# Moving the expert products of tile 0 into the last attention batch of a fused attention, product-key and two-gate expert kernel

## What is computed

```python
x = x + peer(attention(x, cond))          # layer 0
x = x + ffn(moe(x, cond))                 # layer 1
# peer: product keys
q   = batchnorm(a @ w_q)                  # statistics over all 2048 tokens
sim = q . keys                            # 2 x 8 heads x 32 keys for each token
# of the 32 x 32 sums of key scores of a head the best 8 are kept, softmax over them
h   = softmax(scores) * gelu(a @ down_embed[indices].T)
out = h @ up_embed[indices]
# moe: 8 experts, 3 layers, relu, top 2 of a softmax gate;  ffn: 8 experts, 2 layers, gelu, top 2 of a sigmoid gate
```

## Time and profile before

| | |
|---|---|
| median of 3 executions | 784.82 us |
| lowest, highest | 784.77, 787.23 us |
| profiled execution | 787.02 us |
| its span (first to last instruction) | 785.2 us, so 1.8 us lie around it |
| busy share of the span | PE 94%, PEld 83%, ACT 73%, DVE 71%, POOL 40% |
| stages in the span | attention to about 146 us; statistics and folded keys to 162; tiles 0 and 1 by products to 213; first turn to 265; turns in which PE never stops to 785 |

### The profile page before, as it was taken

How to read it: one execution, slowest core, us unless ns; L and a number is a source line. 1 busy time by engine, 2 the same in 40 slices (tenths; PEclk the granted TensorE clock), 3 DMA queues, 4 the chain that set the end, 5 groups by cost and what they waited for, 6 DMA issues and landing times.

```text
span 785.2 us, 14852 instructions
## 1 busy us (share of the span) xinstructions
PE 741.9 (94%) x5314; PEld 654.1 (83%) x5314; DVE 557.1 (71%) x1495; ACT 575.6 (73%) x1001; POOL 312.2 (40%) x214
## 2 busy tenths in 40 slices
PE   6889998979878999999999999999999999999998
PEld 4666767869766799899989989999898899999887
DVE  4887888477379877976977797688679756833422
ACT  3677777369797778978987886897889788553243
POOL 2122222179977175344717543572645161000000
PEclk9999999989997999999999999999999999999999
DMA  8940000000000000000000000000000000000000
GB/s 313 333 117 2 3 1 2 1 1 1 1 1 1 1 1 8 2 1 2 7 1 2 8 1 1 1 8 1 1 5 4 1 1 8 1 1 8 1 1 8
DMA packets 11160, 16.92 MB, mean 22 GB/s; under 512 B 680, under 2 KB 6992, under 8 KB 10832
## 3 DMA queue, kind: packets, MB, share of 16 engines
q1 hardware_dynamic: 10944, 15.72, 6.2%
q10 hardware_dynamic: 144, 0.26, 0.1%
HBM read 14.93 MB, written 1.05 MB: 20 GB/s over the span
## 4 chain that ended last, share of the span: by engine, by line
PE 85%; DVE 6%; ACT 4%; issue 3%; DMA 1%; SPq 0%; DVEq 0%; ACTq 0%
PE banks L448 79%; PE banks L484 4%; ACT G_both L936 2%; PE banks L695 2%; DVE W_both L1444 1%; DMA region<-in_pA 1%; ACT region L1014 1%; DVE acc L1589 1%; PE banks L512 1%; DVE W_both L1213 0%; DVE HF L1450 0%; ACT region L1020 0%; PE banks L727 0%; DVE pairs L1408 0%; DVE top_keys L1403 0%
## 5 line engine op out<-in xcount | busy, mean ns | idle before, releaser
L390 POOL TENSOR_TENSOR region<-sim 128x1024 f32<-128x1024 f32 x128 | 260.8, 2065 | 100.1 <-DVE top_keys L1401 63.2
L1076 ACT ACTIVATE HF<-banks,lpack 128x256 f32<-128x256 f32 x256 | 105.4, 479 | 55.6 <-PE banks L448 54.6
L1014 ACT ACTIVATE region<-region,neg_thr 128x1024 f32<-128x1024 f32 x128 | 143.8, 1153 | 0.0
L1444 DVE SCALAR_TENSOR_TENSOR W_both<-region,rz_rel,W_both 128x1024 f32<-128x1024 f32 x98 | 138.1, 1409 | 1.7
L448 PE MATMUL banks<-HF,w_sb 128*128 128x256 f32 x512 | 124.7, 388 | 7.7 <-DVE HF L1450 7.6
L448 PEld LDWEIGHTS banks<-f_sb,HF 128*128 128x128 f32 x1024 | 123.7, 192 | 3.4
L1020 ACT ACTIVATE region<-region,dtop 128x1024 f32<-128x1024 f32 x114 | 125.3, 1141 | 0.0
L448 PE MATMUL banks<-f_sb,HF 128*128 128x128 f32 x1024 | 124.5, 275 | 0.0
L448 PE MATMUL banks<-cT,f_sb 128*128 128x256 f32 x512 | 122.7, 382 | 0.1
L448 PEld LDWEIGHTS banks<-HF,w_sb 128*128 128x128 f32 x512 | 95.4, 194 | 20.0 <-DVE HF L1450 8.6
L448 PEld LDWEIGHTS banks<-cT,f_sb 128*128 128x128 f32 x512 | 92.1, 190 | 16.3 <-issue 2.9
(11 more groups left out here) (167 smaller groups left out, 1032.7 us busy)
## 6 DMA issues: line engine op xcount, KB each, us to landing
w_sb<-in_w SPq DMA_DIRECT2D x1, 2048.0 KB, 14.0
f_sb<-in_f SPq DMA_DIRECT2D x1, 2048.0 KB, 15.8
region<-in_wq SPq DMA_DIRECT2D x1, 1024.0 KB, 7.9
region<-in_wqT SPq DMA_DIRECT2D x1, 1024.0 KB, 10.0
w_sb<-in_w SPq DMA_DIRECT2D x1, 1024.0 KB, 8.5
out_x<-acc_f SPq DMA_DIRECT2D x16, 64.0 KB, 1.6
x1T_all<-in_xT SPq DMA_DIRECT2D x1, 768.0 KB, 7.7
region<-in_pA SPq DMA_DIRECT2D x1, 588.5 KB, 6.3
```

The lines of the kernel that those rows point to most:

```text
L390: pool.tensor_tensor(S[a][h].rearrange("p (i j) -> p i j", i=NK), sim[a][:, h, :].unsqueeze(2).broadcast_to([P, NK, NK]), sim[a][:, PH + h ...
L1014: act.activation(S[a][h], S[a][h], ACT.Prelu, bias=neg_thr[t % 4][:, h:h + 1], alpha=STEEP).then_inc(h_L, 1)
L1076: m = act.activation(HF[e % 2][:, f, :], bank(2 + b, 256 * (f % 2), 256 * (f % 2) + 256), ACT.Gelu_apprx_tanh, bias=L("bf", 4 * e + f, 4 * ...
L1444: v.scalar_tensor_tensor(W[a], S[a][h], rz_rel[a][:, h:h + 1], W[a], ALU.mult, ALU.add).then_inc(h_w, 1)
```

## The change

Four edits, all between the last attention batch and the first turn:

- Tile 0's 8 expert products are no longer spread over the statistics stage. They stand inside the last attention batch, behind `covariance(2)` and ahead of `out_T(14)`, in banks 3 and 5, and ACT makes their gelu in two instructions of 512 columns right after it has loaded the gelu table.
- The places where tile 0's products stood are now taken by the first six of tile 1's (`second_inputs`); its last two come right behind the products of `weff`, where all 8 of tile 1 stood.
- `mm(bank(6), ones, kb)` moves ahead of the folded keys, which now stand in one piece.
- On ACT, the first `exp_pairs` comes directly behind the first `steep_pairs`, not behind the second.

```diff
-            def first_inputs(a, b):
-
-                if a == 0:
+            def first_inputs(c):
+
+                if c == 0:
                     pe.wait_ge(ld_w, 16 * 8)
                     pe.wait_ge(ld_l, 48)
                     pe.wait_ge(s_x1, 1)
+                for k in range(4):
+                    m = mm(bank(3 + 2 * c, P * k, P * k + P), cols(downT, 4 * c + k), cols(x1T_all, 0))
+                m.then_inc(t_Hp, 1)
+
+            def second_inputs(a, b):
+
+                if a == 0:
+                    pe.wait_ge(s_x1, 2)
                     pe.wait_ge(s_ET, 2 * B)
+                    pe.wait_ge(s_O0, B)
+                    pe.wait_ge(s_O1, B)
                 for k in range(a, b):
-                    m = mm(bank(k // 4, P * (k % 4), P * (k % 4) + P), cols(downT, k), cols(x1T_all, 0))
+                    m = mm(bank(k // 4, P * (k % 4), P * (k % 4) + P), cols(downT, k), cols(x1T_all, 1))
...
                     for t in range(3):
                         covariance(t)
+                    first_inputs(0)
+                    first_inputs(1)
...
-            first_inputs(0, 2)
+            second_inputs(0, 2)
             wait_norm("cov")
+            pe.wait_ge(t_G, 1)
             mm(bank(3, 0, P), cov, A("woT")).then_inc(pe_norm, 1)
...
             mm(bank(7), ones, kb, start=True, stop=False)
-            pe.wait_ge(ld_wqT, 16)
-            folded_keys(0)
-            folded_keys(1)
-            first_inputs(6, 8)
-            folded_keys(2)
             pe.wait_ge(s_x1, B)
             mm(bank(6), ones, kb, start=True, stop=False)
-            folded_keys(3)
+            pe.wait_ge(ld_wqT, 16)
+            for c in range(4):
+                folded_keys(c)
...
-            expert_inputs(1, 1, 0)
-            expert_inputs(1, 1, 1)
+            second_inputs(6, 8)
             expert_inputs(2, 0, 0)
...
             load_table(ACT.Gelu_apprx_tanh, 0)
+            for c in range(2):
+                act.wait_ge(t_Hp, c + 1)
+                m = act.activation(act_of[0][:, 512 * c:512 * c + 512], bank(3 + 2 * c), ACT.Gelu_apprx_tanh)
+            m.then_inc(t_G, 1)
             out_T(B - 1)
...
-            expert_inputs(0, 0)
             act.wait_ge(pe_norm, NORM_PE.index("sim_bias") + 1)
...
             steep_pairs(0, 0, 0)
-            for n in range(18):
+            exp_pairs(0, 0, 0)
+            steep_pairs(0, 0, 1)
+            for n in range(1, 18):
```

More of the change, by code:

```diff
@@ L632, in _ @@
             mm(bank(5, 0, P), A("woT"), cov_w, start=True, stop=False)
-            first_inputs(2, 3)
+            second_inputs(2, 3)
             pe.wait_ge(act_norm, NORM_ACT.index("minus_delta_row") + 1)
             mm(bank(5, 0, P), delta_rows[0:1, 0:P], delta_rows[0:1, P:2 * P], start=False, stop=True).then_inc(pe_norm, 1)
-            first_inputs(3, 6)
+            second_inputs(3, 6)
             def cov_W(c):
```

## The result

| | before | changed |
|---|---|---|
| median of 8 executions | 784.80 us | 788.12 us |
| lowest, highest | 784.51, 787.23 | 786.69, 788.46 |
| profiled execution, its span | 787.02, 785.2 | 787.64, 785.8 |

The ratio is 1.0025, with a 95% interval of 1.0014 to 1.0037: slower by about 2 us. The prediction had 784.3 us and a range up to 787.0; the median lies above it.

The account below looks back on a forecast made before the run. PE was taken to bound the kernel from 320 us on, so only its earlier start counts: -1.13 (last batch's clock) - 0.53 (folded keys) - 0 (ACT's lead) + 1.1 (`peer_out` clock) = -0.56, giving 784.3 us, range 781.7 to 787.0.

Parts of the forecast that it names:

- Part 1, the hole: Last attention batch: tile 0's products fill PE's 1.73 us idle time, the clock holds, values come 1.13 us earlier.
- a rival (0.20): Last attention batch: the clock gain is absent in the median, leaving +0.6 us, 785.4 us; chance 0.20.
- ACT's two gelus: Behind the table load: two gelus, 1.2 us together, hidden in front of ACT's 2.10 us wait for PE.
- Part 2, the folded keys: Folded-key stretch: four records leave, the rest is only reordered without a wait; gain 0.53 us, bounds 0 and 0.53.
- Part 3, ScalarE's lead: ScalarE's start: first `steep_pairs` 3.06 us earlier, a 2.92 us lead from the second head, of which 1.66 us survives.
- ACT's extra lead: At DVE's wait for POOL: ACT's extra 1.26 us are worth nothing, bounds 0 and 1.26.
- The allowance of 0.14 us: ACT's first exponential right behind the `steep_pairs` it reads: 0.14 us allowed, bounds 0 and 0.3.
- The cost at `peer_out`: Tile 1's `peer_out`: longer idle time ahead lowers the clock, costing 1.1 us, bounds 0 and 1.73.
- the foreseen 3.9 us of idle time: Ahead of tile 1's `peer_out`: PE's idle time grows from 2.62 to 3.9 us, with the clock expected low.
- The slower rival: The clock stays down beyond tile 1's `peer_out`: 787.9 us, or 786.8 with the last-batch gain; chance 0.12.
- its 1.9 us for the first expert products: Behind `peer_out`: 8 records of 256 columns take 1.9 us more at the low clock, on DVE's path.
- The sum: Whole change: -1.13 - 0.53 - 0 + 1.1 = -0.56 us, from 784.82 to 784.3 us.

Follow-up runs that it names:

- e15: The kernel before, unedited, one further traced execution: 784.72 us.
- e8: The kernel before with 9 unused products in TensorE's idle time ahead of tile 1's `peer_out`: 786.48 us, ratio 1.0005.
- e13: A further execution of e7's kernel (the kernel before with the last attention batch's hole filled): 787.31 us.
- e14: One more execution of e7's kernel (the kernel before with the last attention batch's hole filled): 786.98 us.
- e7: The kernel before with 8 unused products behind `covariance(2)` in the last attention batch: 786.73 us, ratio 1.0000.
- e1: The changed kernel with the folded keys in their old order, two expert products back among them: 786.72 us, ratio 1.0000.
- e2: The changed kernel with only the constant keys' second product moved between `folded_keys(1)` and `folded_keys(2)`: 786.49 us, ratio 1.0005.
- e4: The kernel before with the four `folded_keys` in one piece, same work in another order: 791.99 us, ratio 1.0073.
- e11: e6 with the first exponential back behind the second `steep_pairs`: 785.25 us, ratio 0.9990.
- e5: The changed kernel itself, measured again: 787.21 us, ratio 1.0022.
- e6: The changed kernel with e2's order and 14 unused products in the idle time ahead of tile 1's `peer_out`: 785.08 us, ratio 0.9989.
- e9: The changed kernel with e2's order and tile 3's key scores one head earlier: 783.55 us, ratio 0.9963.
- e3: The changed kernel with 11 unused products in the idle time ahead of tile 1's `peer_out`: 786.11 us, ratio 1.0003.
- e12: e9 with `keep_x2(1, 1)` and the root on POOL ahead of tile 2's last pair sum: 784.68 us, ratio 0.9984.
- e16: The kernel before, unedited, another traced execution: 787.10 us.
- e10: The kernel before with only tile 3's key scores one head earlier: 786.12 us, ratio 0.9994.

## Why the prediction was wrong

**Part 1, the hole: right in the trace, wrong in the time.** The products fit (idle 0, `out_T` on time), the clock held and the values came 1.16 us earlier, foreseen 1.13. But I kept that as a gain of the whole. In the lower group of executions there is no fall to be saved (e15, e8); in the upper group the clock falls at `peer_out` instead (e13, e14). e7 measures the term as 0 (0.9988 to 1.0012). I had named the first half of this as a rival (0.20), not the second. ACT's two gelus were hidden as foreseen: B is 20.19 in e1 with them, 20.22 before.

**Part 2, the folded keys: the step that failed.** It reads "The rest is only put in another order, and the order lets no wait in [...] Gain 0.53; bounds 0 and 0.53." The order let no wait in. It let the clock fall without one: 32 records of 32 columns in one piece, then `weff` in 3.75 us for 1.95. B became 1.0 to 1.5 us longer than before, where I had 0.5 less. e1 and e2 take the fall away (e2 with nothing but order), and e4 puts it into the kernel before. I had looked for a fall only behind idle time, and gave no rival to this part and no loss to its bounds.

**Part 3, ScalarE's lead: right.** In e2 the first `steep_pairs` starts at 167.12 (foreseen 167.0), the second exponential at 171.44 (171.3), and nothing of ACT's extra lead arrives: DVE loses it in the wait for POOL, and e11 shows the exchange of the exponentials to be worth 0. The allowance of 0.14 us had no row behind it; in e2 the first exponential starts 1.18 us behind the first `steep_pairs`, where an instruction of ACT has 1.04. In the first trace of the changed kernel ScalarE was late too and the wait short (0.88 us); in e5 DVE's instruction took 1.77.

**The cost at `peer_out`: right.** +1.52 us in the first trace, +0.95 in e5, for +1.1. In e6 against e2, C says 1.51. The clock did not need the foreseen 3.9 us of idle time: it fell behind 2.81 in the first trace (3.70 in e5).

**The slower rival: near in time, wrong in mechanism.** It had 787.9 us, close to the median of 788.12, and my range ended below it. But its 1.9 us for the first expert products is not there: in e5, e1 and e13 the clock stays low for 10 us, far beyond `peer_out`, and from the end of `peer_out` to `sum_T` it still takes 52.0 us, before 51.9. That the number fits is luck.

**The sum.** Against C of before, the changed kernel has +3.0 and +2.1 in its two traces. I had -0.53 + 1.1 = +0.6 for that stretch. Of the difference, 1.5 to 2.0 us are the missing 0.5 and the fall behind the keys, up to 0.4 the size of the fall at `peer_out` (in e5 it was 0.15 smaller than foreseen). With A's 1.16 not counting in the median, 2.1 to 3.0 us are 0.27 to 0.39% against the measured 0.25 (0.14 to 0.37). The forecast of 784.3 stood besides on a median of three of the lower group; in the later sets the kernel before has 786.35 to 786.57.

## What to carry to other kernels

Look at what TensorE does ahead of a fall of its clock, not only at how long it rests: here 32 narrow records in one piece brought it down while the busy share said 1.00, and one wide product between them kept it up. When an idle time is filled, ask at which later one the clock may fall instead, and take a gain in the clock from several traces or from an edit of its own, since one trace shows one moment of it. When one engine's lead ends in a wait for another's long instruction, it is worth something only in whole instructions of that one (e9: 1.87 us).

## What the runs showed of the hardware

- The clock fell with TensorE busy without a gap: at 158.1 us, among 32 records of 32 columns that run from 154.8 to 158.6 (changed kernel; e4 at 160.6). In e5 it fell at 158.8, in the 0.56 us of idle time behind such a piece, in e3 at 160.8, 0.6 us into the products behind it. With one product of 512 columns in the middle it stayed at 1.00 (e2, e6, e9, e11, e12).
- The same idle time of 2.62 us left the clock up (e15, e16) or brought it down (e13, e14), and that of 1.73 us too (down in the first trace and e16, up in e15).
- DVE's pair sums took 0.69 us when they met POOL's gap and 1.7 to 2.5 when POOL was in an instruction (e2, e9, e10). `peer_out` of tile 1 started 46.3 us behind POOL's first pair sum in fifteen of eighteen traces, one instruction of POOL earlier in e9 and e12 (44.5) and one later in e4 (48.2), never in between.
- The executions of one program lie in two groups about 2 us apart. In e15 and e16 the whole 2.38 us are differences in the moments at which the clock changes. What sets these moments for an execution stays open.
